# A fused transformer layer with self and cross attention: where the row maxima stand in a hand-written order

## The chip, the cores and the metric

The kernel runs on one core of a Trainium2 chip. The metric is the device time of one execution in microseconds, the median of several runs. The engines that matter here: TensorE (PE) multiplies matrices into PSUM banks, VectorE (DVE) and ScalarE (ACT) read the banks, GpSimd (POOL) works on small SBUF tiles, and SyncE (SP) issues all DMAs in one queue. Each engine runs its own instructions in order and waits on semaphores.

## What is computed

A layer on 16 sequences of 112 rows with 256 features, and 16 source sequences of 375 rows. There are 16 heads of 16 features. The reference, cut down:

```python
x = _layernorm(tgt, ln1_g, ln1_b)
q, k, v = (_heads(t) for t in jnp.split(x @ sa_wqkv, 3, axis=-1))
wei = jnp.einsum('bhtd,bhsd->bhts', q, k) * scale
wei = jnp.where(causal[None, None], wei, NEG_INF)
wei = jnp.where(tgt_padding_mask[:, None, None, :], NEG_INF, wei)
wei = jax.nn.softmax(wei, axis=-1)
sa_out = _merge(jnp.einsum('bhts,bhsd->bhtd', wei, v)) @ sa_wproj + sa_bproj
result = tgt + sa_out
xq = _layernorm(result, ln2_g, ln2_b)
xs = _layernorm(src, ln2_g, ln2_b)
k2, v2 = (_heads(t) for t in jnp.split(xs @ ed_wkv, 2, axis=-1))
q2 = _heads(xq @ ed_wq)
wei2 = jax.nn.softmax(jnp.einsum('bhtd,bhjd->bhtj', q2, k2) * scale, axis=-1)
ed_out = _merge(jnp.einsum('bhtj,bhjd->bhtd', wei2, v2)) @ ed_wproj + ed_bproj
result = result + ed_out
h = jax.nn.relu(_layernorm(tgt, ln3_g, ln3_b) @ ff_w1 + ff_b1)
result = result + (h @ ff_w2 + ff_b2)
```

## The kernel before

The 16 sequences are worked off in 4 groups of 4. Each group has 8 units of attention: units 0 to 3 are the self attention of its four sequences, units 4 to 7 the cross attention of the same four. The units follow each other in the order 2, 3, 4, 5, 0, 1, 6, 7, where 0 and 1 belong already to the next group; so the program repeats one period per group, with a start in front and a last group without successors behind.

A unit has four quarters of four heads. A quarter's scores are one bank of PSUM for a self unit (112 keys) and three for a cross unit (three chunks of 125 keys). The scores leave PE with their row maximum already subtracted: the maximum is computed first, from a separate pass of matmuls, and enters the score matmul as extra rows of the stacked operands. The steps of the order, by their names in the code:

- `max`: PE multiplies into one of three banks `mxb` (four heads at once for a self unit, L1011 and L1015; one head for a cross unit, L1018), and DVE reduces the bank to negated maxima `negm` (L845 self, L848 cross). A self unit has 4 such steps, a cross unit 16. PE waits for DVE when it comes back to a bank (`MAX_BANKS` is 3).
- `max_parts`: POOL splits the maxima of half a unit (8 heads) into three bf16 parts, in four small operations that depend on each other (L638, L640, L642, L644), once the half's last maximum is reduced.
- `mT`: PE transposes these parts into a bank of `misc` (L1062), and ACT copies them, spread over the columns, into `q1st` or `q2st` (L710, 0.91 us each).
- `score` (L1029, L1034), the exponential on ACT into `prob` (L719), `pv`, the weighted sum (L1050), `ot`, its copy by ACT (L726), then `o1` (a transpose, L1057, divided by DVE into `att`, L852 and L854), `o2` (a transpose, L1068, copied by ACT into `aT`) and `o3` (the output projection, L1086, added on DVE; for a cross unit it is followed by the store).
- `qk1`, `q2`, `k2`: projections in three matmul passes twice (L936, L937, L938). The result is split into three bf16 parts, the first on ACT (L704), the other two by three DVE operations (L782 into `rem`, L784, L786). SP then stacks them with 6 DMAs per half (`stack_q1`, `stack_q2`, `stack_k2`). `v1`, `v2`: value projections, copied by ACT.
- `sT`, `xT`, `xq`: transposes of normalised rows (`xs`, `xn`, `xr`), stored as a high part by ACT and a low part by DVE (L775, L832). `stats...` and `norm...` are the layer norms, on DVE with two POOL operations between. `ff1` and `ff2` are the feed-forward matmuls (L1079 for the second).
- `load_tb` and `resid`: the residual's rows come by DMA and POOL adds a bias (L628); `o3` of a self unit adds onto them on DVE (L865).

All steps but scores, maxima and weighted sums use the two banks `misc` in turn, in the order of the steps (`misc_bank`). So a step waits for the reader of the last but one step of this kind.

The order is written by `period_steps`. `other_work` is a table: for each quarter (unit, quarter) a list of other steps. For every quarter three lists are dealt out in turn: its own scores with the weighted sum of the quarter before and an `mT` whose parts are ready; maxima ahead; and the other work. Before, the maxima beside a quarter are those of the quarter four further on, that is of the next unit:

```python
ahead = maxima(*quarters[(n + LEAD) % len(quarters)])
heads = [g] if u < BG else range(4 * g, 4 * g + 4)
```

So a cross unit's sixteen maxima stand four to a quarter beside the unit in front, also where that is a self unit with a single score per quarter: unit 4's beside unit 3, unit 6's beside unit 1. A self unit's four maxima stand one to a quarter. `program_steps` lays the periods behind each other and gives each step the group that it belongs to. Every engine goes through the same list and issues its part of each step.

## Time and profile before

| | us |
|---|---|
| median of 3 runs | 630.61 (628.57 to 631.55) |
| the profiled execution, its own time | 630.3 |
| its span in the trace | 628.4 |

The trace gives every instruction's start and duration on its engine and, for an idle time of an engine, the instruction elsewhere that ended it. Matmuls overlap, so the time that a step takes PE is read from its start to the next start. Units were placed by the order of the instructions: in the second period the first halves or quarters named below run from 211.25 (unit 7), 235.64 (unit 2), 248.96 (unit 3), 273.07 (unit 4), 285.89 (unit 5), 306.88 (unit 0), 321.66 (unit 1), 334.18 (unit 6) and 352.74 (unit 7 again).

### The profile page before, as it was taken

The page shows a single profiled execution, that of the slowest core. Times are in us where ns is not written, and L with a number is a line of the kernel's source. Part 1 is how long each engine was busy: PE and PEld are TensorE (multiplying, and loading weights), DVE is VectorE, ACT ScalarE, POOL GpSimd, SP SyncE. Part 2 cuts the span into 40 slices and gives each one's busy share as a digit, 9 for nine tenths or more (in the row PEclk, how much of TensorE's full clock was granted, in tenths as well). Part 3 has the DMA queues.
Part 4 walks back from the last instruction along what each step waited for, and adds up shares of the span by engine and source line. Part 5 has one row for each costly group of instructions (what it writes and reads, how often), then busy time and mean ns, then how long its engine had stood idle before and what let it go on. Part 6 is the DMA issues. An engine that isn't in the chain of part 4 may idle for free.

```text
span 628.4 us, 14141 instructions
## 1 busy us (share of the span) xinstructions
PE 553.9 (88%) x5564; PEld 448.0 (71%) x5564; DVE 415.1 (66%) x982; ACT 325.3 (52%) x613; POOL 128.9 (21%) x370
## 2 busy tenths in 40 slices
PE   3497899898999999898998999898999999989896
PEld 3395577776877777777876777776877777767664
DVE  5975376788557656698557656698558654685571
ACT  2141646446645756447635756446635655376173
POOL 6800222113103212113112212113112211030010
PEclk9997999999999999999999999999999999999998
DMA  8297018596562038395481039295670058104910
GB/s 244 75 125 141 4 34 128 97 113 72 112 121 64 2 85 132 56 130 66 109 128 47 1 88 131 55 126 68 113 126 20 8 96 131 40 2 79 117 15 16
DMA packets 73122, 52.08 MB, mean 83 GB/s; under 512 B 21920, under 2 KB 72288, under 8 KB 73056
## 3 DMA queue, kind: packets, MB, share of 16 engines
q1 hardware_dynamic: 73056, 51.17, 49.2%
q8 instruction: 44, 0.72, 0.6%
q14 instruction: 22, 0.18, 0.1%
HBM read 14.36 MB, written 1.84 MB: 26 GB/s over the span
## 4 chain that ended last, share of the span: by engine, by line
PE 53%; DVE 26%; ACT 9%; issue 5%; DMA 4%; POOL 3%; SPq 1%; DVEq 0%; POOLq 0%; ACTq 0%
DVE negm L848 8%; PE misc L936 7%; PE misc L1079 7%; PE pvb L1050 6%; PE misc L938 5%; PE scb L1034 5%; PE misc L937 5%; DVE rem L782 3%; PE misc L1086 3%; DMA tb<-in_x 3%; PE mxb L1018 3%; ACT prob L719 2%; ACT qkp L704 2%; DVE stats L758 1%; PE misc L1057 1%
## 5 line engine op out<-in xcount | busy, mean ns | idle before, releaser
L719 ACT ACTIVATE prob<-scb 125x448 f32<-125x448 f32 (+1 forms) x256 | 134.1, 543 | 66.8 <-PE scb L1034 63.0
L848 DVE TENSOR_REDUCE negm<-mxb 112x1 f32<-112x375 f32 x256 | 128.8, 539 | 24.2 <-PE mxb L1018 22.5
L1018 PE MATMUL mxb<-k2st,q2st 96*112 96x375 bf16 x256 | 82.2, 337 | 5.6 <-DVE negm L848 5.1
L1034 PE MATMUL scb<-q2st,k2st 128*125 128x112 bf16 x768 | 74.7, 223 | 4.9 <-ACT prob L719 4.2
L1034 PEld LDWEIGHTS scb<-q2st,k2st 128*125 128x125 bf16 x768 | 64.8, 137 | 17.7 <-ACT prob L719 9.7
L638 POOL CAST mparts<-negm 112x8 bf16<-112x8 f32 x64 | 12.2, 191 | 313.2 <-DVE negm L845 159.6
L845 DVE TENSOR_REDUCE negm<-mxb 112x4 f32<-112x448 f32 x64 | 39.4, 618 | 45.8 <-PE mxb L1015 45.8
L704 ACT ACTIVATE qkp<-misc,bcol 128x224 bf16<-128x224 f32 (+2 forms) x64 | 35.6, 558 | 62.9 <-PE misc L938 51.7
L1050 PE MATMUL pvb<-prob,v 125*17 125x112 f32 (+1 forms) x2048 | 65.0, 261 | 0.1
L782 DVE SCALAR_TENSOR_TENSOR rem<-misc,bcol,qkp 128x224 f32<-128x224 f32 (+2 forms) x64 | 37.5, 587 | 40.4 <-ACT qkp L704 39.7
L1079 PE MATMUL misc<-wf,hT 128*112 128x256 f32 x256 | 59.6, 380 | 0.9 <-DVE rem L782 0.9
L1050 PEld LDWEIGHTS pvb<-prob,v 125*17 125x17 f32 (+1 forms) x2048 | 44.2, 97 | 15.2 <-issue 11.4
L1079 PEld LDWEIGHTS misc<-wf,hT 128*112 128x112 f32 x256 | 44.4, 177 | 11.4 <-DVE rem L782 2.1
L1018 PEld LDWEIGHTS mxb<-k2st,q2st 96*112 96x112 bf16 x256 | 32.1, 130 | 19.2 <-DVE negm L848 13.0
L710 ACT ACTIVATE q1st<-misc 24x896 bf16<-24x896 f32 x32 | 29.1, 910 | 21.1 <-PE misc L1062 20.6
L689 ACT ACTIVATE hT<-misc,bcol 128x448 f32<-128x448 f32 x32 | 20.3, 635 | 32.8 <-PE misc L938 32.8
L710 ACT ACTIVATE q2st<-misc 24x896 bf16<-24x896 f32 x32 | 29.1, 910 | 15.2 <-PE misc L1062 14.5
L936 PE MATMUL misc<-wv_hi,xsT_hi 128*125 128x256 f32 x96 | 31.4, 328 | 5.1 <-DVE rem L782 3.6
L786 DVE TENSOR_TENSOR qkp<-rem,qkp 128x224 bf16<-128x224 f32 (+2 forms) x64 | 34.0, 531 | 2.2
L698 ACT ACTIVATE v<-misc 125x256 f32<-125x256 f32 x48 | 18.5, 385 | 26.4 <-PE misc L938 26.0
L1034 PEld LDWEIGHTS scb<-q1st,k1st 128*112 128x112 bf16 x256 | 23.6, 132 | 5.8 <-issue 0.2
L617 POOL TENSOR_TENSOR veps<-mv,epst 112x1 f32<-112x1 f32 (+2 forms) x36 | 7.0, 194 | 100.8 <-DVE mv L762 100.8
(149 smaller groups left out, 1206.1 us busy)
## 6 DMA issues: line engine op xcount, KB each, us to landing
k2st<-qkp SPq DMA_DIRECT2D x192, 93.8 KB, 4.5
xs<-in_ctx SPq DMA_DIRECT2D x16, 375.0 KB
q1st<-qkp SPq DMA_DIRECT2D x48, 112.0 KB, 5.6
k1st<-qkp SPq DMA_DIRECT2D x48, 112.0 KB, 7.6
q2st<-qkp SPq DMA_DIRECT2D x96, 56.0 KB, 2.2
xn<-in_x SPq DMA_DIRECT2D x4, 448.0 KB, 7.2
tb<-in_x SPq DMA_DIRECT2D x8, 224.0 KB, 9.6
out<-ostage SPq DMA_DIRECT2D x16, 112.0 KB, 4.5
```

The costliest lines, as they stand in the source:

```text
L704: nc.scalar.activation(parts_of(s)[:, 0, 0:n], misc_bank(s)[:, 0:n], ACT.Identity, bias=bcol[:, col:col + 1]).then_inc(s_p1, 1)
L710: nc.scalar.activation(rows, bank[NROW:NROW + 3 * HH, 0:T].unsqueeze(1).broadcast_to([3 * HH, HH, T]), ACT.Copy).then_inc(s_read["act"], 1)
L719: nc.scalar.activation(prob[0:rows, n % PROB_SLOTS, :], scb[n % SCORE_BANKS][0:rows, 0:GH * T], ACT.Exp, scale=SCALE).then_inc(s_ex, 1)
L782: V.scalar_tensor_tensor(r[:, 0:n], bank[:, 0:n], bias, parts[:, 0, 0:n], ALU.add, ALU.subtract).then_inc(s_read["dve"], 1)
L786: V.tensor_tensor(parts[:, 2, 0:n], r[:, 0:n], parts[:, 1, 0:n], ALU.subtract).then_inc(s_p3, 1)
L845: V.tensor_reduce(negm[:, at, i * GH:(i + 1) * GH], mx[0:T, 0:GH * T].rearrange("p (h s) -> p h s", h=GH), axis=AX_X, op=ALU.max, negate=T ...
L848: V.tensor_reduce(negm[:, at, i:i + 1], mx[0:T, 0:S], axis=AX_X, op=ALU.max, negate=True).then_inc(s_mx, 1)
L936: M(dst, w_hi[:, k], x_hi[:, k], start=(k == 0), stop=False)
L1018: mm = M(mx[0:T, 0:S], q2st[0:NROW, i, b * T:(b + 1) * T], k2st[k2_place(q, b)][0:NROW, i, 0:S], start=True, stop=True)
L1034: mm = M(sc[0:rows, j * T:(j + 1) * T], ks, (q1st if u < BG else q2st)[:, h, b * T:(b + 1) * T], start=(u >= BG), stop=(u >= BG or j == GH ...
L1050: mm = M(pvb[32 * j:32 * j + VW, g * T:(g + 1) * T], vals, prob[0:rows, slot, j * T:(j + 1) * T], start=(c == 0), stop=(c == chunks(u) - 1))
L1079: mm = M(bank[0:T, 0:C], hT[:, f, b * T:(b + 1) * T], wf2[:, f, :], start=(f == 0), stop=(f == FT - 1))
```

## The change

A table `MAXIMA_BESIDE` takes the place of `LEAD`: for each unit and quarter it names the unit whose maxima stand there, and which. The self units' maxima stand two to a quarter beside the cross unit in front of the pair: all eight of units 0 and 1 beside unit 5, all eight of units 2 and 3 beside unit 7. The sixteen maxima of unit 4 stand two to a quarter beside units 2 and 3, those of unit 6 beside units 0 and 1. Units 5 and 7 keep theirs beside 4 and 6.

With it, other work moves. `o2` and `o3` of unit 7 go from the end of the period into the first quarter of unit 2 of the next (`o2_late`, `o3_late`, with `of_period` giving them the right group). In unit 7 the projection `q2` comes ahead of `sT`, each K projection is followed by its stack sooner, and `ff1` 3 stands last. In unit 5 the first K projection moves ahead of `xq` 3.

```diff
-LEAD = 4
+MAXIMA_BESIDE = {2: ((4, 0, 1), (4, 2, 3), (4, 4, 5), (4, 6, 7)), 3: ((4, 8, 9), (4, 10, 11), (4, 12, 13), (4, 14, 15)),
...
-        (2, 0): [("load_tb", 1), [("sT", 1, 0), ("sT", 1, 1)]],
+        (2, 0): [("o2_late", 7), ("load_tb", 1), [("sT", 1, 0), ("sT", 1, 1)], ("o3_late", 7)],
...
-        (5, 0): [[("sT", 2, 0), ("sT", 2, 1)], ("xq", 3), ("stats_s", 3)],
-        (5, 1): [("q2", 1, 0), ("stack_q2", 1, 0), ("o1", 4), ("k2", 2, 0), ("stack_k2", 2, 0), ("q2", 1, 1), ("stack_q2", 1, 1), ("k2", 2, 1), ("stack_k2", 2, 1)],
+        (5, 0): [[("sT", 2, 0), ("sT", 2, 1)], ("k2", 2, 0), ("xq", 3), ("stack_k2", 2, 0), ("stats_s", 3)],
+        (5, 1): [("q2", 1, 0), ("stack_q2", 1, 0), ("o1", 4), ("q2", 1, 1), ("stack_q2", 1, 1), ("k2", 2, 1), ("stack_k2", 2, 1)],
...
-        (7, 0): [[("sT", 0, 0), ("sT", 0, 1)]],
-        (7, 1): [("q2", 0, 0), ("stack_q2", 0, 0), ("o1", 6), ("q2", 0, 1), ("stack_q2", 0, 1), ("k2", 0, 0), ("ff1", 3), ("k2", 0, 1)],
+        (7, 0): [("q2", 0, 0), ("stack_q2", 0, 0), [("sT", 0, 0), ("sT", 0, 1)], ("q2", 0, 1)],
+        (7, 1): [("k2", 0, 0), ("stack_k2", 0, 0), ("stack_q2", 0, 1), ("o1", 6), ("k2", 0, 1), ("stack_k2", 0, 1), ("ff1", 3)],
         (7, 2): [("o2", 6), ("stats_s", 1), ("v2", 0, 0), ("v2", 0, 1)],
-        (7, 3): [("o3", 6), [("stack_k2", 0, 0), ("stack_k2", 0, 1)], ("norm_s", 1), ("v2", 0, 2), ("load_src", 2)],
+        (7, 3): [("o3", 6), ("norm_s", 1), ("v2", 0, 2), ("load_src", 2)],
...
     def maxima(u, g):
-        heads = [g] if u < BG else range(4 * g, 4 * g + 4)
-        return [[("max", u, i)] for i in heads] + ([[("max_parts", u, g // 2)]] if g % 2 else [])
+        of, *numbers = MAXIMA_BESIDE[u][g]
+        half = 2 if of < BG else H // 2
+        return [[("max", of, i)] for i in numbers] + ([[("max_parts", of, numbers[-1] // half)]] if (numbers[-1] + 1) % half == 0 else [])
...
-            ahead = maxima(*quarters[(n + LEAD) % len(quarters)])
+            ahead = maxima(u, g)
...
-    s += [("pv", u, 3, c) for c in range(chunks(u))] + [("ot", u), ("v1", 2), ("o1", u), ("v1", 3), ("o2", u), ("o3", u)]
+    s += [("pv", u, 3, c) for c in range(chunks(u))] + [("ot", u), ("v1", 2), ("o1", u), ("v1", 3)]
...
+    def of_period(t, R):
+        kind, *rest = t
+        if kind == "load_tgt":
+            return ("load_tgt", R + 1, *rest)
+        if kind.endswith("_late"):
+            return (kind[:-len("_late")], R - 2, *rest)
+        return (kind, R if t in head else R - 1, *rest)
```

Line numbers behind the table are 14 higher in the changed kernel (L1018 becomes L1032, L1062 becomes L1076). Three places of the order follow.

PE in unit 3 of the second period, round `mT` of unit 4's first half. Before, with `mparts` written by POOL, `att` by DVE, `aT` not yet needed:

```order
L1029 MATMUL scb0<-maskt,identb 112x448
L1034 MATMUL scb0<-q1st,k1st 112x112 x4
L1018 MATMUL mxb2<-k2st0,q2st 112x375
L1068 MATMUL misc1<-ident,att 128x112 x2
L1062 MATMUL misc0<-identb,mparts0 24x112
L1018 MATMUL mxb0<-k2st0,q2st 112x375
L936 MATMUL misc1<-xT_hi,wqk_hi 128x448
```

and now, a quarter earlier:

```order
L952 MATMUL misc0<-xT_hi,wf1_lo 128x448
L1076 MATMUL misc1<-identb,mparts0 24x112
L1043 MATMUL scb1<-maskt,identb 112x448
L1048 MATMUL scb1<-q1st,k1st 112x112 x4
L1032 MATMUL mxb1<-k2st0,q2st 112x375
L1071 MATMUL misc0<-ident,ot 112x128 x4
L1032 MATMUL mxb2<-k2st0,q2st 112x375
```

The `mT` moved from behind `o2` in the third quarter to behind a hidden projection in the first, while its maxima moved a whole unit forward.

PE in unit 0, behind the second K projection of unit 3 of the group before (`k2`, then `v2`). Before:

```order
L938 MATMUL misc0<-xsT_hi,wk2_lo 128x376
L1029 MATMUL scb0<-maskt,identb 112x448
L1034 MATMUL scb0<-q1st,k1st 112x112 x4
L1011 MATMUL mxb2<-identb,maskt 112x448
L1015 MATMUL mxb2<-k1st,q1st 112x112 x4
L1062 MATMUL misc1<-identb,mparts0 24x112
L936 MATMUL misc0<-wv2_hi,xsT_hi 125x256
```

and now:

```order
L952 MATMUL misc0<-xsT_hi,wk2_lo 128x376
L1043 MATMUL scb0<-maskt,identb 112x448
L1048 MATMUL scb0<-q1st,k1st 112x112 x4
L1032 MATMUL mxb2<-k2st0,q2st 112x375
L1032 MATMUL mxb0<-k2st0,q2st 112x375
L950 MATMUL misc1<-wv2_hi,xsT_hi 125x256
```

The `mT` is gone from here, so the value projection writes the other bank of `misc`, and two cross maxima stand where one self maximum stood.

DVE in unit 7, first half, behind the first self maximum. Before, with `rem` and `qkp` the splits of `q2` (128x224) and `k2` (128x375), and `rden`, `att` those of `o1`:

```order
L845 TENSOR_REDUCE negm<-mxb2 112x4
L782 SCALAR_TENSOR_TENSOR rem<-misc1,bcol,qkp 128x224
L784 CAST qkp<-rem 128x224
L786 TENSOR_TENSOR qkp<-rem,qkp 128x224
L852 RECIPROCAL rden<-misc0 112x16
L854 TENSOR_TENSOR att<-misc0,rden 112x256
L782 SCALAR_TENSOR_TENSOR rem<-misc1,bcol,qkp 128x224
L784 CAST qkp<-rem 128x224
L786 TENSOR_TENSOR qkp<-rem,qkp 128x224
L782 SCALAR_TENSOR_TENSOR rem<-misc0,bcol,qkp 128x375
```

and now:

```order
L796 SCALAR_TENSOR_TENSOR rem<-misc1,bcol,qkp 128x224
L798 CAST qkp<-rem 128x224
L800 TENSOR_TENSOR qkp<-rem,qkp 128x224
L859 TENSOR_REDUCE negm<-mxb0 112x4
L796 SCALAR_TENSOR_TENSOR rem<-misc1,bcol,qkp 128x375
L798 CAST qkp<-rem 128x375
L800 TENSOR_TENSOR qkp<-rem,qkp 128x375
L859 TENSOR_REDUCE negm<-mxb1 112x4
L866 RECIPROCAL rden<-misc0 112x16
L868 TENSOR_TENSOR att<-misc0,rden 112x256
L796 SCALAR_TENSOR_TENSOR rem<-misc0,bcol,qkp 128x375
```

The division of `o1` moved from behind one split to behind three (the first stands just above this piece), with the self maxima between them.

## Rows read from the trace of the kernel before

**Rows 1.** of the page: busy time, share of the span and instructions by engine
```profile
PE 553.9 (88%) x5564; PEld 448.0 (71%) x5564; DVE 415.1 (66%) x982; ACT 325.3 (52%) x613; POOL 128.9 (21%) x370
```

**Rows 2.** by windows: stretch, its length, then busy us by engine, granted clock, DMA share
```profile
211.25:223.19 11.94, 11.00 (x124) 9.06 (x125) 8.06 (x20) 7.99 (x16) 1.57 (x8) 1.00 0.10 26
...
256.99:265.54 8.55, 7.46 (x41) 6.16 (x40) 4.89 (x10) 2.72 (x5) 0.79 (x4) 1.00 0.14 45
...
285.89:297.69 11.80, 9.86 (x122) 8.11 (x120) 9.63 (x27) 7.69 (x16) 3.43 (x11) 1.00 0.34 49
```

**Rows 3.** timelines of PE round mT of unit 4: start, us, instruction, [idle before <-releaser]
```profile
119.52 0.21 PE L1062 MATMUL misc<-identb,mparts 112*24 112x112 bf16 x1 [1.25 <-POOL mparts L644]
...
258.99 0.21 PE L1062 MATMUL misc<-identb,mparts 112*24 112x112 bf16 x1 [1.09 <-POOL mparts L644]
...
538.96 0.21 PE L1062 MATMUL misc<-identb,mparts 112*24 112x112 bf16 x1 [1.52 <-POOL mparts L644]
```

**Rows 4.** timeline of PE in unit 0: the V projections of unit 3
```profile
315.09 0.39 PE L936 MATMUL misc<-wv_hi,xsT_hi 128*125 128x256 f32 x1 [1.03 <-DVE rem L782]
...
316.54 0.38 PE L936 MATMUL misc<-wv_hi,xsT_hi 128*125 128x256 f32 x1 [0.28 <-ACT v L698]
```

**Rows 5.** timeline of PE in the last group, units 5 to 6
```profile
580.68 0.62 PE L1057 MATMUL misc<-ident,ot 128*112 128x128 f32 x4 [0.81 <-ACT ot L726]
...
589.75 0.64 PE L1018 MATMUL mxb<-k2st,q2st 96*112 96x375 bf16 x3
...
592.00 1.03 PE L1086 MATMUL misc<-wpe,aT 128*112 128x256 f32 x4
...
596.64 0.32 PE L1018 MATMUL mxb<-k2st,q2st 96*112 96x375 bf16 x1
...
598.30 0.41 PE L936 MATMUL misc<-wv_hi,xsT_hi 128*125 128x256 f32 x1
```

**Rows 6.** by form, DVE: line, tiles, shapes, count | busy us, mean ns | idle before
```profile
L848 DVE TENSOR_REDUCE negm<-mxb 112x1 f32<-112x375 f32 x256 | 128.8, 539 | 24.2 <-PE mxb L1018 22.5
L845 DVE TENSOR_REDUCE negm<-mxb 112x4 f32<-112x448 f32 x64 | 39.4, 618 | 45.8 <-PE mxb L1015 45.8
L782 DVE SCALAR_TENSOR_TENSOR rem<-misc,bcol,qkp 128x375 f32<-128x375 f32 x32 | 19.4, 608 | 22.6 <-ACT qkp L704 22.0
```

**Rows 7.** timeline of PE in unit 3, second quarter: transpose behind o1
```profile
255.02 0.60 PE L951 MATMUL misc<-ident,xn 112*128 112x112 f32 x4 [0.63 <-DVE att L854]
```

**Rows 8.** timeline of DVE at the end of unit 1: residual sum
```profile
336.22 0.42 DVE L865 TENSOR_TENSOR tb<-misc,tb 112x256 f32<-112x256 f32 x1 [2.48 <-POOL tb L628]
```

**Rows 9.** timeline of PE, end of unit 7 and start of unit 2
```profile
234.71 1.09 PE L1086 MATMUL misc<-wpe,aT 128*112 128x256 f32 x4 [0.54 <-ACT aT L712]
...
237.77 0.43 PE L971 MATMUL misc<-ident,xs 125*128 125x125 f32 x2 [0.55 <-ACT q1st L710]
```

**Rows 10.** timeline of DVE in unit 7, first half
```profile
212.40 0.38 DVE L832 TENSOR_TENSOR xq_lo<-misc,xq_hi 128x224 fp32r<-128x224 f32 x1
...
213.24 1.24 DVE L775 TENSOR_TENSOR xsT_lo<-misc,xsT_hi 128x375 fp32r<-128x375 f32 x2
...
218.90 0.42 DVE L854 TENSOR_TENSOR att<-misc,rden 112x256 f32<-112x256 f32 x1
```

**Rows 11.** timeline of PE in unit 5: second K projection
```profile
296.54 0.44 PE L936 MATMUL misc<-xsT_hi,wk_hi 128*128 128x376 f32 x1 [0.62 <-DVE rem L782]
```

**Rows 12.** by windows at the start, columns as in rows 2
```profile
60.00:63.00 3.00, 3.00 (x18) 2.69 (x17) 0.62 (x1) 0.77 (x2) 0.78 (x4) 0.50 0.34 114
```

**Rows 13.** timeline of PE at the start: one self maximum, then mT
```profile
62.85 0.58 PE L1011 MATMUL mxb<-identb,maskt 112*112 112x448 bf16 x1
...
63.59 0.22 PE L1062 MATMUL misc<-identb,mparts 112*24 112x112 bf16 x1
```

**Rows 14.** timeline of SyncE's queue: issues of a K stack
```profile
229.75 8.88 SPq L543 DMA_DIRECT2D k2st<-qkp  x12
```

**Rows 15.** by tile, k2st: time from issue to landing
```profile
DMA to landing us min/median/max: 3.3/4.7/7.4
```

More of the change, by code:

```diff
@@ L52 @@
 FF2_PIECES = 2
-LEAD = 4
+MAXIMA_BESIDE = {2: ((4, 0, 1), (4, 2, 3), (4, 4, 5), (4, 6, 7)), 3: ((4, 8, 9), (4, 10, 11), (4, 12, 13), (4, 14, 15)),
+                 4: tuple((5,) + tuple(range(4 * g, 4 * g + 4)) for g in range(4)), 5: ((0, 0, 1), (0, 2, 3), (1, 0, 1), (1, 2, 3)),
+                 0: ((6, 0, 1), (6, 2, 3), (6, 4, 5), (6, 6, 7)), 1: ((6, 8, 9), (6, 10, 11), (6, 12, 13), (6, 14, 15)),
+                 6: tuple((7,) + tuple(range(4 * g, 4 * g + 4)) for g in range(4)), 7: ((2, 0, 1), (2, 2, 3), (3, 0, 1), (3, 2, 3))}
 MISC_READER = {"xT": "dve", "qk1": "dve", "v1": "act", "ff1": "act", "sT": "dve", "k2": "dve", "v2": "act", "ff2": "dve",
@@ L158, in of_next @@
         if kind in ("max", "max_parts", "mT", "score", "pv", "ot", "o1", "o2", "o3", "stats2", "norm2", "xq"):
-            return t[1] in (0, 1) or (t[1] == UNITS[0] and kind in ("max", "max_parts", "mT") and at[t] > len(s) // 2)
+            return t[1] in (0, 1) or (t[1] in UNITS[:2] and kind in ("max", "max_parts", "mT") and at[t] > len(s) // 2)
         if kind in ("q2", "stack_q2"):
@@ L173, in program_steps @@
     steps, head = period_steps(kt)
-    placed = [("load_tgt", 0)] + [(t[0], R + 1 if t[0] == "load_tgt" else R if t in head else R - 1) + t[1:]
-                                  for R in range(groups + 1) for t in steps]
+    def of_period(t, R):
[5 more added lines that the diff above has]
+        return (kind, R if t in head else R - 1, *rest)
+    placed = [("load_tgt", 0)] + [of_period(t, R) for R in range(groups + 2) for t in steps]
     return [t for t in placed if 0 <= t[1] < groups]
```

## The prediction

> **What bounds the kernel now.** I read the page's busy rows first [rows 1]: TensorE (PE) is busy 88% of the span, VectorE (DVE) 66%. What to see is that no other engine comes near, and that the change can only act on the gaps of TensorE, since it adds and removes no arithmetic. Next the table by stretches [rows 2]: in the steady part a period of about 140 us repeats three times, and its stretches differ. In the third quarter of unit 3 (256.99 to 265.54) PE is busy 7.46 of 8.55 us while DVE works only 4.89; in the first half of unit 5 (285.89 to 297.69) PE is busy 9.86 of 11.80 and DVE 9.63; in the first half of unit 7 (211.25 to 223.19) DVE has 8.06 of 11.94. So DVE is no bound on average but is close to one in the two halves to which the change adds self maxima. Last the timelines round PE's longest waits [rows 3 to 5, 7 to 11]: who releases PE, and how long it stood.
>
> **The change, part by part.** The program's matmuls, reductions, exponentials and DMAs keep their number and shapes, so each term is a wait that goes or comes. The sum is made on the profiled execution's own time, 630.3 us (span 628.4 and 1.9 around it), which lies 0.3 us under the median of 630.61.
>
> 1. *Unit 4's first eight maxima are ready sooner.* Before, the matmul that turns the parts of unit 4's maxima (mT) stands only a score, one maximum and o2 behind the eighth of these maxima, and PE waits for the last of four POOL operations: 1.25, 1.09, 1.09 and 1.52 us, once in each group (the two middle ones alike, one is shown) [rows 3]. Afterwards the eight maxima end in the last quarter of unit 2, and unit 3's first score, a weighted sum and a hidden projection stand between, which lies over the POOL chain of four operations. What is late next is qk1, whose operands are ready. Gain 4.9 us; 3.5 if DVE's norm1, which now comes behind the eighth maximum, is taken to delay it.
>
> 2. *Unit 0, behind unit 3's K projections.* Before, mT takes a bank of misc between the second K projection and the first V projection, so V needs the bank that DVE's rem operation reads last: 1.03 us, then 0.28 for the next one, in three groups [rows 4]. Afterwards mT stands a unit earlier, V takes the other bank, and only the transpose behind V meets the later rem. PE arrives there some 0.6 us before DVE is done, so about half of 1.31 stays; leaving out the order of banks, the bounds are a gain of 0 and of 1.31 each. I take 0.8 three times: 2.4.
>
> 3. *Last group.* Before, with no work of a next group, unit 6's sixteen maxima stand nearly bare: the first six take PE from 589.75 to 592.00, at DVE's pace, and five later ones with mT from 596.64 to 598.30 [rows 5]. Afterwards six of them stand in unit 5's tail, where PE waits 0.81 us for ot and again for rem anyway. The first cluster falls from 2.25 us to nothing, the second from 1.66 to about 1.1: gain 2.8. Bounds: 0.5 (DVE, at 539 ns a maximum [rows 6], becomes late for the rems) to 3.5.
>
> 4. *Residual's landing.* At the end of unit 1, DVE waits for the sum that POOL makes of a DMA just landed: 2.48 us in one group [rows 8], and less in the two others. Between that load and its reader three fewer cross maxima stand afterwards (1.1 us less cover on PE), but as DVE also has no maximum left to do behind it, PE may run about 1.7 us further, until its three maximum banks are full. I take a gain of 0.6 in two of the three groups, rounded up for the third: 1.3. Bounds: loss 2, gain 2.5.
>
> 5. *o2 and o3 of unit 7 moved into the next unit.* PE's wait for aT goes (0.54 us, and some 0.3 of waiting that the overlap of matmuls hides in the row), three times. In exchange o2 and o3 now share two misc banks with mT and two transposes; the second transpose waited 0.55 us for the 0.91 us copy of mT before [rows 9], and now the first one also waits for aT and o3 for the first one's xsT_lo: about 0.6 more. Net gain 0.2 each: 0.6, bounds ±2.
>
> 6. *Fewer maxima at a time in units 1, 2 and 3.* DVE does 8 cross maxima in unit 3 instead of 16, so norm1, att and rem stand less behind them. The two behind o1 in unit 3 show in [rows 7] as 0.63 for att and a shorter one; with others like them in the three units I take 0.8 a group: 2.5, rounded up. Bounds 0 and 4.5.
>
> 7. *Unit 7's first half, the price.* Two more self maxima, at 618 ns on DVE each, and two stacks' projections sooner [rows 6]. The q2 projection now comes right behind the first maximum, at 211.9, and needs xq_lo, which DVE ends at 212.78 [rows 10]: 0.9 us. Its second half wants the bank that xsT_lo frees, 0.8 later. The second K projection wants the bank of att, and att now stands behind two splits for q2, one for K and three self maxima. DVE's queue from 214.2 on, added up: q2 split 1.1, maximum 0.6, two xsT_lo 1.2, q2 split 1.1, maximum 0.6, K split 1.5, maximum 0.6, rden and att 0.7 [rows 6, 10], where a split's cast and subtraction together are taken at one and a half times its rem operation: 7.4, and 1.5 of standing for ScalarE's first parts, so 223.1. PE comes at 221.8: 1.3 to 1.4. Walked through to its end with these durations, the half ends at 225.3 instead of 223.19; 0.8 of that is the two maxima's own matmuls, which unit 2 no longer has. Net loss 1.3, three times: 3.9. Bounds: 0 to 8.
>
> 8. *Unit 5's first half, the price.* Two more self maxima in a stretch where DVE has 9.63 of 11.80 [rows 2]. The wait of 0.62 for rem [rows 11] is replaced by a like one; xq and q2 come 0.5 later behind the K split, and the bank of o1 some 0.6 later behind DVE's queue; walked through, the half ends at 299.5 instead of 297.69, of which 0.95 is work moved here. Net loss 0.85, three times: 2.5. Bounds 0 to 5.
>
> 9. *Start.* All eight self maxima of units 0 and 1 before the first score. From 60 to 63 PE's granted clock is 0.50, 1.2 GHz of its 2.4, behind a stretch in which it had little to do; at that clock a self maximum takes PE 0.74 us from start to next start (62.85 to 63.59) [rows 12, 13], more than DVE's 618 ns, so that the new order, which by the same adding up would save 2 us at full clock, saves 0.6. Bounds: ±2.
>
> Sum: −4.9 −2.4 −2.8 −1.3 −0.6 −2.5 +3.9 +2.5 −0.6 = −8.7, and 630.3 − 8.7 = 621.6.
>
> The new waits are many and short. In the stretches of rows 2 the granted clock stays at 1.00, although PE stands there for up to 1.09 us at a time [rows 2, 3]. The Trainium skill (TensorE: Matmul & The Clock Gate, "A second HAM failure mode: psum-queue depth-cycling") says that frequent micro-idles between groups of matmuls can make the clock fall and rise again; this trace does not show it. By that rule the new waits of unit 7 could bring it about; that is one of the rivals.
>
> **The rivals.**
> - *Waits only move to DVE.* In units 5 and 7 the queue is longer than I added up, so terms 7 and 8 cost double: +6.4, 628.0 us. For: DVE's 9.63 of 11.80 [rows 2], and every delay there is queued in front of the next reader of a bank. Against: the quarters behind them have slack, and DVE's idle share is over 30% in unit 7.
> - *The losses don't come.* A wait of PE for one engine overlaps one for another, so terms 7 and 8 vanish and the rest stays: 615.2.
> - *Slower: unit 4's stack lands too late.* The first cross maximum now comes at about 236.9 instead of 249.36. Before, twelve issues for that stack ran from 229.75 over 8.88 us, and a landing takes 3.3 to 7.4 us [rows 14, 15]. Afterwards its first half is issued from about 222, behind six issues of a q stack, and has landed by 226 + 7.4 = 233.4, 3.5 us early. It decides once the K split ends more than 3.5 us later, or a landing doubles under the loads. A maximum 4 us late would stop PE in four places: +16, 637.6 us.
> - *The clock falls.* A stretch at 0.50 like the start's [rows 12] in unit 7 of each of three groups, taken at twice the 3 us shown, would cost half its length: +9 to +10, 631.7. Against: no stretch of rows 2 shows one.
> - *Nothing moves in effect:* the order shows every place changed, so this needs gains and prices that cancel: 630.3.
>
> **How the numbers follow.** Forecast 0.55 (616 to 627); waits moved to DVE 0.22; losses absent 0.10; late stack 0.07; clock 0.03; nothing 0.03. The time is the forecast's 621.6. The range takes in the first three cases nearly whole, with the bounds of terms 3, 7 and 8: 612.5 to 630, leaving out late stack, clock and the ends of the others, some 0.2. A change of 0.5% is about what a measurement of this kernel can tell: 3.2 us, faster below 627.5. Faster: 0.55 + 0.10 + 0.05 of the second = 0.70; same: 0.17 + 0.03 + 0.02 = 0.22; slower 0.08.
>
> **What would show it.** Right: mT of unit 4 has no wait for POOL; V behind unit 3's K projections waits under 0.1 us; from ff2 of the last group to unit 6's first score is 2 to 3 us shorter; in unit 7's first half a K projection waits over 1 us for att. Wrong: the first cross maximum of unit 4 waits for a DMA; PE's share of unit 5 falls under 80%; the clock row of the page shows a second low stretch; DVE waits over 3 us for POOL's residual.

## The result: slower by 1.1%, and the profile after

The changed kernel takes 637.41 us (median; 634.59 to 640.44), the kernel before 629.59 in the same series; the ratio is 1.0113, with a 95% interval of 1.0077 to 1.0148. The forecast was 621.6 us, and faster. The profiled execution of the changed kernel has a span of 635.2 us, 6.8 more than before.

The page of the changed kernel, its busy time by engine and the granted clock in 40 slices:

```profile
PE 551.2 (87%) x5564; PEld 445.9 (70%) x5564; DVE 416.9 (66%) x982; ACT 324.8 (51%) x613; POOL 132.6 (21%) x370
...
PEclk9966898999999999999999999999999999999999
```

Against [rows 1] PE is busy 2.7 us *less*: no work was added, and the loss of 6.8 us is standing time of PE. The same stretches as in [rows 2], by windows of the changed kernel (stretch, length, busy us of PE, PEld, DVE, ACT, POOL, granted clock, DMA share): first half of unit 7, third quarter of unit 3, first half of unit 5.

```profile
216.37:231.18 14.81, 11.85 (x134) 9.91 (x135) 9.35 (x23) 8.72 (x17) 2.33 (x12) 1.00 0.20 48
265.09:271.88 6.79, 6.79 (x39) 5.86 (x38) 3.13 (x6) 1.81 (x4) 0.00 (x0) 1.00 0.13 44
292.07:306.15 14.08, 11.13 (x133) 9.08 (x131) 11.50 (x31) 8.58 (x17) 4.12 (x15) 1.00 0.53 76
```

What to see: unit 3's quarter fell from 8.55 to 6.79 us and PE no longer stands in it at all. Unit 7's half rose from 11.94 to 14.81 and unit 5's from 11.80 to 14.08. The first half of unit 7 was given 25.3 - 23.2 = 2.1 us more by the prediction; it took 2.9. The waits that it named are there, in the timeline of PE (start, us, instruction, idle before and its releaser):

```profile
218.05 0.34 PE L950 MATMUL misc<-xq_hi,wq_hi 128*128 128x224 f32 x1 [0.84 <-DVE xq_lo L846]
...
222.00 0.37 PE L950 MATMUL misc<-xq_hi,wq_hi 128*128 128x224 f32 x1 [0.71 <-DVE xsT_lo L789]
...
228.84 0.44 PE L950 MATMUL misc<-xsT_hi,wk_hi 128*128 128x376 f32 x1 [1.22 <-DVE att L868]
```

What the prediction did not have stands in the first group. There unit 7's projections and self maxima run with no unit 7 beside them, between unit 1's last score and unit 2's first. This stretch, before and after, by windows:

```profile
72.24:95.86 23.62, 21.20 (x165) 17.19 (x163) 16.30 (x45) 10.61 (x22) 6.50 (x14) 1.00 0.12 30
```

```profile
72.72:102.44 29.72, 23.72 (x186) 19.53 (x184) 19.30 (x52) 12.52 (x24) 8.99 (x26) 0.97 0.25 50
```

It is 6.1 us longer, of which 1.6 is four self maxima moved here from unit 2, and some 0.9 is the granted clock (an estimate: 3% of 29.7 us at 0.97). PE's timeline there, and POOL's queue behind its longest wait:

```profile
87.49 0.37 PE L950 MATMUL misc<-xq_hi,wq_hi 128*128 128x224 f32 x1 [1.19 <-DVE xsT_lo L789]
...
91.30 0.44 PE L950 MATMUL misc<-xsT_hi,wk_hi 128*128 128x376 f32 x1 [0.86 <-DVE rem L796]
...
99.82 0.21 PE L1076 MATMUL misc<-identb,mparts 112*24 112x112 bf16 x1 [1.88 <-POOL mparts L658]
```

```profile
97.66 0.85 POOL L633 TENSOR_TENSOR rstd<-veps,mhalf 125x3 f32<-125x3 f32 x1
98.47 0.19 POOL L652 CAST mparts<-negm 112x8 bf16<-112x8 f32 x1
...
99.42 0.25 POOL L658 TENSOR_TENSOR mparts<-mrem,mparts 112x8 bf16<-112x8 f32 x1
```

The POOL wait that the change removed in unit 3 has a new place: the parts of unit 3's maxima are queued behind `rstd`, which waits for DVE's statistics, which stand behind two maxima; and PE has nothing to do there but V projections that come before `mT`.

Where the 6.8 us went, by the starts of the units' first scores in both traces: up to unit 1's last score +0.5; to unit 2 +6.1; units 2 and 3 of the first group -2.9; then, summed over three passes each, units 7, 2 and 3 +2.9, and units 4, 5, 0, 1 and 6 +1.5; from the last group's unit 4 on -1.4.

### The profile page after: what moved, and what is told of

It reads as the page before. It is cut to its first block, busy times and chain, and to the rows that moved or that the text cites. A ratio compares the mean times of both kernels' runs of the same rounds, so it can differ in the third digit from the quotient of the medians.

```text
span 635.2 us, 14143 instructions
## 1 busy us (share of the span) xinstructions
PE 551.2 (87%) x5564; PEld 445.9 (70%) x5564; DVE 416.9 (66%) x982; ACT 324.8 (51%) x613; POOL 132.6 (21%) x370
## 4 chain that ended last, share of the span: by engine, by line
PE 53%; DVE 23%; ACT 10%; DMA 5%; issue 4%; SPq 3%; POOL 2%; DVEq 0%; POOLq 0%; ACTq 0%
PE misc L950 8%; PE misc L1093 7%; PE pvb L1064 7%; PE misc L952 6%; PE misc L951 5%; DVE negm L862 5%; PE scb L1048 5%; DVE rem L796 4%; PE mxb L1032 3%; PE misc L1100 3%; DMA tb<-in_x 3%; ACT qkp L718 2%; ACT prob L733 2%; SPq L557 2%; DVE qkp L800 2%
## 5 line engine op out<-in xcount | busy, mean ns | idle before, releaser
L862 DVE TENSOR_REDUCE negm<-mxb 112x1 f32<-112x375 f32 x256 | 130.7, 540 | 43.8 <-PE mxb L1032 41.2
L1032 PE MATMUL mxb<-k2st,q2st 96*112 96x375 bf16 x256 | 82.8, 336 | 1.9 <-DVE negm L862 1.7
L718 ACT ACTIVATE qkp<-misc,bcol 128x375 bf16<-128x375 f32 (+2 forms) x64 | 35.6, 558 | 73.8 <-PE misc L952 62.4
L652 POOL CAST mparts<-negm 112x8 bf16<-112x8 f32 x64 | 16.7, 261 | 269.3 <-DVE negm L862 166.9
L796 DVE SCALAR_TENSOR_TENSOR rem<-misc,bcol,qkp 128x375 f32<-128x375 f32 (+2 forms) x64 | 37.5, 586 | 47.8 <-ACT qkp L718 47.4
L1064 PE MATMUL pvb<-prob,v 125*17 125x112 f32 (+1 forms) x2048 | 66.4, 263 | 0.6 <-ACT prob L733 0.2
L1093 PE MATMUL misc<-wf,hT 128*112 128x256 f32 x256 | 58.1, 380 | 1.4 <-DVE rem L796 1.4
L1032 PEld LDWEIGHTS mxb<-k2st,q2st 96*112 96x112 bf16 x256 | 32.4, 130 | 11.9 <-DVE negm L862 6.5
L800 DVE TENSOR_TENSOR qkp<-rem,qkp 128x375 bf16<-128x375 f32 (+2 forms) x64 | 33.9, 530 | 2.2
L1025 PE MATMUL mxb<-identb,maskt 112*112 112x448 bf16 x64 | 25.3, 395 | 7.3 <-DVE edb L940 2.8
```

The costliest lines, as they stand in the source:

```text
L718: nc.scalar.activation(parts_of(s)[:, 0, 0:n], misc_bank(s)[:, 0:n], ACT.Identity, bias=bcol[:, col:col + 1]).then_inc(s_p1, 1)
L796: V.scalar_tensor_tensor(r[:, 0:n], bank[:, 0:n], bias, parts[:, 0, 0:n], ALU.add, ALU.subtract).then_inc(s_read["dve"], 1)
L800: V.tensor_tensor(parts[:, 2, 0:n], r[:, 0:n], parts[:, 1, 0:n], ALU.subtract).then_inc(s_p3, 1)
L862: V.tensor_reduce(negm[:, at, i:i + 1], mx[0:T, 0:S], axis=AX_X, op=ALU.max, negate=True).then_inc(s_mx, 1)
L1032: mm = M(mx[0:T, 0:S], q2st[0:NROW, i, b * T:(b + 1) * T], k2st[k2_place(q, b)][0:NROW, i, 0:S], start=True, stop=True)
L1064: mm = M(pvb[32 * j:32 * j + VW, g * T:(g + 1) * T], vals, prob[0:rows, slot, j * T:(j + 1) * T], start=(c == 0), stop=(c == chunks(u) - 1))
```

## Experiments

**The two halves of the edit, and the two pairs.** The work order alone (every maximum as before):

```diff
-MAXIMA_BESIDE = {2: ((4, 0, 1), ...), 3: ..., 5: ..., 0: ..., 1: ..., 7: ...}
+MAXIMA_BESIDE = {2: ((3, 0), (3, 1), (3, 2), (3, 3)), 3: tuple((4,) + tuple(range(4 * g, 4 * g + 4)) for g in range(4)), ...}
```

> The other work of the changed kernel (unit 7's and unit 5's projections in the new order, o2 and o3 of unit 7 in the next unit), with every maximum placed as before. Theory M (the price comes from the two extra self maxima standing in the same half as the projections, because each takes DVE time and holds up the reader of the next misc bank): unit 7's first half in the steady part lies near before's 11.9 us plus at most 0.7, the waits for POOL in units 3 and for the V projection in unit 0 come back, and the whole is 630 to 633 us. Rival W (the new order of the projections alone is the price: q2 in front of the transposes, K ahead of the second stack): the first half of unit 7 stays at 14 us or so as in the changed kernel, the gains in units 3 and 0 are missing, and the whole is 639 to 644 us.

Measured: 636.95 us, ratio 1.0088 (1.0058 to 1.0119). This is between the two ranges. For the whole, theory M falls: without a single moved maximum the kernel is as slow as the changed one. Its first halves of units 7 and 5, and two of the waits in unit 7:

```profile
209.29:222.26 12.97, 10.92 (x124) 9.08 (x125) 8.74 (x22) 7.70 (x16) 1.55 (x8) 1.00 0.15 36
285.50:298.28 12.78, 9.99 (x120) 8.24 (x119) 9.94 (x28) 7.67 (x16) 3.32 (x11) 1.00 0.44 70
```

```profile
210.97 0.34 PE L954 MATMUL misc<-xq_hi,wq_hi 128*128 128x224 f32 x1 [0.84 <-DVE xq_lo L850]
...
214.62 0.37 PE L954 MATMUL misc<-xq_hi,wq_hi 128*128 128x224 f32 x1 [0.81 <-DVE xsT_lo L793]
```

Each half is 1.0 us longer than before with the same work in it, and rival W's 14 us for unit 7's half is not reached either. Of the 2.9 us that this half grew by in the changed kernel, the order makes 1.0; with the maxima alone (next run) it is 13.54 us, 1.6 longer, of which 0.8 is moved work. So both halves of the edit have a price there. By rows of this execution, the span of 635.1 is made up of before's 628.4, +4.7 in units 7 and 2, +3.2 in unit 5, +2.2 in the last group's unit 5 and +1.7 in its unit 3, in both of which the granted clock fell, +0.7 between the first group's unit 1 and unit 2, -3.1 in unit 6's first quarters, -2.5 by an earlier first score, and -0.2 in the rest.

The maxima alone:

```diff
-        (7, 0): [("q2", 0, 0), ("stack_q2", 0, 0), [("sT", 0, 0), ("sT", 0, 1)], ("q2", 0, 1)],
+        (7, 0): [[("sT", 0, 0), ("sT", 0, 1)]],
...
-        (7, 3): [("o3", 6), ("norm_s", 1), ("v2", 0, 2), ("load_src", 2)],
+        (7, 3): [("o3", 6), [("stack_k2", 0, 0), ("stack_k2", 0, 1)], ("norm_s", 1), ("v2", 0, 2), ("load_src", 2)],
```

> All maxima placed as in the changed kernel, but the other work as before, so that the K stack of unit 4 is issued in unit 7's last quarter, near 230 us, while the first cross maximum for it stands in unit 2's first quarter. If the sooner stacks are needed, TensorE stands for a DMA at the first cross maximum of unit 4, 5 to 10 us in each of four groups: 650 to 670 us. Rival (stacks land in time anyway, and theory W holds): no DMA wait over 1 us there, and the whole is under before, 622 to 628 us, since it has all gains and no reordered projections.

Measured: 632.07, ratio 1.0031 (1.0001 to 1.0062). Neither number is met. The stacks land in time even when issued late: over the whole trace PE waits for them twice, 2.0 us in all, both times in the last group (by tile, `k2st`):

```profile
who waited for it (us, times):
  PE mxb L1032: 2.0, 2
```

So "stacks filled sooner" bought almost nothing, and the order it needed cost 1.0 us a half. In the steady part the moved maxima of units 2 to 4 about cancel (unit 7 +3.0, units 2 and 3 -2.9), and those of units 0, 1 and 6 gain 0.65 a group. What keeps the whole above before is the first group's stretch, 29.78 us here as well, with a POOL wait of 2.94 in it. With the work order alone it was 24.30, so the price of the first group comes mostly with the self maxima that stand there, not with the order:

```profile
97.48 0.21 PE L1076 MATMUL misc<-identb,mparts 112*24 112x112 bf16 x1 [2.94 <-POOL mparts L658]
```

The change in units 7, 2, 3 alone, and in units 5, 0, 1 alone (table rows and work of the other pair as before):

> The change in units 7, 2 and 3 alone (self maxima of units 2 and 3 beside unit 7, o2 and o3 of unit 7 late, unit 4's stack sooner); units 5, 0 and 1 as before. From the rows of the changed kernel: unit 7's first half costs 1.9 us net three times, the same stretch of the first group, where nothing stands beside it, 4.5 net (6.1 longer, 1.6 of it moved work), unit 2 some 0.3 each, and unit 3 gives back 1.0 four times: 5.7 + 4.5 + 1.0 - 4.0 = +7, 634 to 638 us. If this half of the change is not to blame: under 631 us.

Measured: 635.89, ratio 1.0090 (1.0059 to 1.0121), inside its range.

> The change in units 5, 0 and 1 alone (self maxima of units 0 and 1 beside unit 5, unit 2's first K projection in unit 5's first quarter, unit 6's maxima spread over units 0 and 1); units 7, 2 and 3 as before. From the rows of the changed kernel: unit 5's first half +1.3 net three times, unit 0 -1.0 three times, unit 1 -0.3 three times, the last group's tail -2: 4.0 - 3.0 - 0.9 - 2.0 = -2, 626 to 630 us. If this half costs as much as the other: over 632 us.

Measured: 631.34, ratio 1.0036 (0.9997 to 1.0075), 1.3 us over before where a gain was expected within 626 to 630; why it missed was not followed. Together the two make the whole loss (+5.8 and +1.3 against +7.8); four fifths of it is the pair of units 7, 2 and 3.

**The first group's order undone.** The list of steps is taken from the kernel before up to unit 4's first score in the first group:

```diff
+    a, b = program_steps_a(kt, groups), program_steps_b(kt, groups)
+    first = ('score', 0, 4, 0, 0)
+    return b[:b.index(first)] + a[a.index(first):]
```

> The changed kernel, with the order of the kernel before up to the first score of unit 4 of the first group, and its own order from there. Theory F: a fixed price is paid once, in the first group, where unit 7's stretch has no unit 7 beside it: from its first maximum to unit 2's first score the changed kernel took 19.8 us against 13.7, of which 1.6 is moved work and 2.9 is given back in units 2 and 3. The stretch is then 13.7 again and the whole 3 to 4 us shorter than the changed kernel's 637.4: 633.5 to 634.5 us. Rival (the start of this execution was slow for its low clock alone, by chance): the whole stays within 1 us of the changed kernel, 636.5 to 638.5.

Measured: 634.34 us, ratio 1.0092 (1.0063 to 1.0121), inside theory F's range, 3.1 under the changed kernel. The two medians come from different series, each with its own runs of before (629.41 and 629.59), and the intervals of the two ratios overlap; the difference of 3.1 alone would not show the theory. The stretch does: it is 23.6 us with the order of before there, as in the kernel before, and 29.6 to 29.8 in the changed kernel, the run with the maxima alone and that with units 7, 2 and 3 alone.

**Two `mT` steps moved, nothing else.**

```diff
+MOVED = ((('mT', 4, 0), ('qk1', 2)), (('mT', 1, 0), ('v2', 3, 1)))
...
+    for t, behind in MOVED:
+        s.remove(t)
+        s.insert(s.index(behind) + 1, t)
```

> The kernel before, in which only two mT steps move later in their quarter: that of unit 4's first half from behind o2 of unit 2 to behind the last qk1 of the quarter, and that of unit 1's first half from in front of unit 3's V projections to behind them. Theory G (the gains of terms 1 and 2 need no other place of the maxima): the wait for POOL in unit 3 (1.09 to 1.52 us, four times) and the wait of V for rem in unit 0 (1.31 in all, three times, about half of it kept) go: 630.1 - 4.9 - 2.4 = 622.8, taken with 623 to 626. Rival (other waits take their place, since the quarters' length is set by DVE's maxima and splits): 629 to 631.

Measured: 625.68, ratio 0.9910 (0.9869 to 0.9952). Theory G holds, inside its range, with no maximum moved. The whole gains 3.7 us, half of the 7.3 that terms 1 and 2 promised. The third and the fourth quarter of unit 3:

```profile
257.41:264.79 7.38, 7.38 (x42) 6.05 (x40) 4.80 (x10) 1.86 (x5) 0.79 (x4) 1.00 0.16 50
264.79:272.93 8.14, 7.47 (x39) 5.87 (x39) 6.48 (x13) 3.31 (x5) 0.00 (x0) 1.00 0.79 109
```

The third went from 8.55 to 7.38; the fourth gave 0.6 back (7.52 before). Unit 0's third quarter went from 4.40 to between 3.31 and 3.35 and gave nothing back. By the rows, units 3 and 0 together gain 6.1 us in this execution, and unit 6's first quarters, where the residual is waited for, take 4.0 of it away: 7.35, 6.45 and 5.92 us in place of 4.35, 6.37 and 4.96. The residual's load lands there in 7.0 to 7.5 us; before it did in 5.4 to 7.4.

**o2 and o3 of unit 7 late, alone** (the rest as before).

```diff
-        (2, 0): [("load_tb", 1), [("sT", 1, 0), ("sT", 1, 1)]],
+        (2, 0): [("o2_late", 7), ("load_tb", 1), [("sT", 1, 0), ("sT", 1, 1)], ("o3_late", 7)],
```

> The kernel before, with o2 and o3 of unit 7 moved into unit 2's first quarter and nothing else. If the price read in the run with the other work alone is this step's (unit 7's last quarter 8.57 to 7.03 us, unit 2's first 2.51 to 4.59, together +0.54 a group): +0.5 three times, 631 to 632 us. If the move is a gain of 0.2 each as forecast: 629.5. If it is the whole price of the new work order in unit 7 (+1.5 a group): 634 to 635.

Measured: 629.92, ratio 0.9993 (0.9959 to 1.0028). From unit 7's last quarter to the end of unit 2's first the trace of this kernel has 11.26 us, that of before 11.08: +0.2 a group, neither the gain of 0.2 nor the loss of 0.5. PE's waits there were 0.54 for `aT` and 0.55 for `mT`'s copy; now they are 0.30, 0.39 and 0.55, for `aT`, that copy and the transposes' low part.

```profile
227.67:238.93 11.26, 10.02 (x115) 7.68 (x115) 4.87 (x14) 7.26 (x14) 1.92 (x6) 1.00 0.57 90
```

**The parts that the rows had shown to gain, together:** the maxima of units 0, 1 and 6 as changed, every projection as before, `mT` of unit 4 late.

> The kernel before with two parts: the maxima of units 0, 1 and 6 placed as in the changed kernel (beside units 5, 0 and 1) while every projection keeps its old place, and mT of unit 4's first half behind the last qk1 of its quarter. From the rows of the run with the maxima alone, units 5, 0 and 1 gain 0.65 a group and the last group's tail 1.3 to 2; the mT step gains 1.1 to 1.5 four times if theory G holds: 630.1 - 2.0 - 1.6 - 4.6 = 622, taken with 621 to 625 us. If theory G falls: 626 to 628.

Measured: 625.01, ratio 0.9911 (0.9882 to 0.9940), at the head of its range. That is no better than the two `mT` steps alone, whose ratio is 0.9910.

**All maxima moved, first group and projections as before.**

> All maxima placed as in the changed kernel, the projections in the order of before, and the first group up to its unit 4 in the order of before throughout. The run with the maxima alone took 632.1 us; the first group's price, 3 to 4 us by the run that undid it, goes: 628 to 629.5 us. If the gains and prices of the maxima cancel in each period as the rows of that run say (unit 7 +3.0, units 2 and 3 -2.9, units 5, 0 and 1 -0.65), it can't come below 627. If the maxima table was a gain throughout and only the start spoilt it: 624 to 626.

Measured: 629.08, ratio 0.9996 (0.9958 to 1.0034). This is inside the first range. With the first group's order and the work order as before, the whole table of maxima is worth nothing measurable.

**The residual's load sooner** (term 4), on the kernel before:

```diff
+MOVED = ((('load_tb', 0), ('score', 0, 3, 0)),)
```

> The kernel before, with the load of the residual's first half issued at the start of unit 0's last quarter, some 7 us sooner, and nothing else. Theory L (term 4's wait is the landing of this load, which POOL's sum waits for with DVE or the parts of unit 6's maxima queued behind it): unit 6's first quarter falls from 4.35, 6.37 and 4.96 us to 4.2 each, 3 us in all: 626.5 to 628 us. Rival (the wait is for POOL's queue or the DMA engines, which an earlier issue doesn't change): 629 to 631.

Measured: 628.16, ratio 0.9954 (0.9920 to 0.9988). Unit 6's first quarter is 4.23 us in all three groups, as expected, but not for the reason expected. SyncE's queue in this kernel, then in the one before:

```profile
327.31 0.32 SPq L558 DMA_DIRECT2D tb<-in_x  x1
327.68 0.36 SPq L563 DMA_DIRECT2D xs<-in_ctx  x1
```

```profile
322.12 0.49 SPq L558 DMA_DIRECT2D xs<-in_ctx  x1
326.96 0.35 SPq L573 DMA_DIRECT2D out<-ostage  x1
327.35 0.43 SPq L553 DMA_DIRECT2D tb<-in_x  x1
```

The load is issued at 327.3 in both. What changed is that the load of source rows (375 KB) now comes behind it and not 5 us ahead of it, and a store of 112 KB behind it as well; which of the two matters was not separated. The residual's load lands in 2.6 us instead of 7.4, and in the two other groups in 3.3 and 2.9 instead of 5.4 and 6.0. By tile `tb`, of this kernel and of before in that stretch:

```profile
DMA to landing us min/median/max: 2.6/2.6/2.6
```

```profile
DMA to landing us min/median/max: 7.4/7.4/7.4
```

**The transposes ahead of q2 again** in unit 7, the rest as changed:

```diff
-        (7, 0): [("q2", 0, 0), ("stack_q2", 0, 0), [("sT", 0, 0), ("sT", 0, 1)], ("q2", 0, 1)],
+        (7, 0): [[("sT", 0, 0), ("sT", 0, 1)], ("q2", 0, 0), ("stack_q2", 0, 0), ("q2", 0, 1)],
```

> The changed kernel, with the two transposes of unit 7's first quarter ahead of both q2 projections again (as before) and the rest as changed. Theory Q (the price of the new work order in unit 7 is that q2 needs DVE's low part of xq at once, 0.57 us, and that its second half wants the bank of DVE's low part of the transposes, 0.66 to 1.19 us): unit 7's first half falls by about 1 us in each of three groups and in the first: 633 to 634.5 us against 637.4. Rival (it is the K projections and stacks that come sooner, with two splits more in DVE's queue): 636.5 to 638.

Measured: 632.86, ratio 1.0044 (1.0010 to 1.0078), 4.5 us under the changed kernel. Theory Q holds, a little under its range. The half is 13.54 us in place of 14.81; the waits for `xq_lo` and `xsT_lo` are gone but for 0.16, that for `att` stays. The first group's stretch is 27.87 us in place of 29.72, about half of it because the granted clock is 1.00 there in this execution:

```profile
211.48:225.02 13.54, 11.85 (x134) 9.76 (x135) 9.45 (x23) 8.71 (x17) 2.34 (x12) 1.00 0.19 48
```

```profile
222.68 0.44 PE L950 MATMUL misc<-xsT_hi,wk_hi 128*128 128x376 f32 x1 [1.22 <-DVE att L868]
```

**The mix with three more moves.**

```diff
+MOVED = ((('mT', 4, 0), ('qk1', 2)), (('load_tb', 0), ('score', 0, 3, 0)), (('mT', 0, 0), ('k2', 2, 1)), (('mT', 3, 0), ('v2', 1, 1)))
```

> The mixed kernel (625.0 us: maxima of units 0, 1 and 6 as changed, projections as before, mT of unit 4 late) with three more moves: the residual's load sooner, mT of unit 0's first half behind unit 2's second K projection, and mT of unit 3's first half behind unit 1's second V projection. If the waits add up one by one: -3.0 for the load, -0.6 three times and -0.4 four times: 625.0 - 6.4 = 618.6, taken with 618 to 621 us. If the removed waits come back at the next bank: 623 to 625.

Measured: 623.04, ratio 0.9873 (0.9814 to 0.9931): between the two cases. The load's move brought unit 6's first quarter to 4.11 us; the two moves of `mT` brought their waits back at the next bank: in unit 5 the 1.20 us for `rem` at q2 became 0.50, 0.17 and 0.40 for later ones, and unit 2's third quarter went from 5.89 to 6.13.

**Three prices undone together** (first group, transposes first, unit 5's order), the rest as changed:

> The changed kernel with three things undone together: the first group's order up to its unit 4, the transposes ahead of q2 in unit 7, and unit 5's projections in the order of before. If the prices found one by one add up: q2's place 4.5 us, of which 1.5 lies in the first group and is counted there, the first group 3.1 to 3.7, unit 5's order 1.0 three times: 637.4 - 3.0 - 3.4 - 3.0 = 628, taken with 626.5 to 629. If they overlap (each wait hides another): 631 or more.

Measured: 626.91, ratio 0.9956 (0.9926 to 0.9986), inside its range. The prices add up, and what remains of the change is a gain of 0.4%.

**Unit 5's order alone**, on the kernel before:

```diff
-        (5, 0): [[("sT", 2, 0), ("sT", 2, 1)], ("xq", 3), ("stats_s", 3)],
+        (5, 0): [[("sT", 2, 0), ("sT", 2, 1)], ("k2", 2, 0), ("xq", 3), ("stack_k2", 2, 0), ("stats_s", 3)],
```

> The kernel before, with unit 5's projections in the changed order and nothing else (the first K projection of unit 2 and its stack in unit 5's first quarter). By the rows of the run with the other work alone, unit 5's first half goes from 11.8 to 12.8 us in each of three groups and in the last group too by about 1: 629.5 + 3 to 4 = 632.5 to 633.5. If that price belonged to the other moves: within 1 us of 629.5.

Measured: 630.36, ratio 1.0017 (0.9984 to 1.0051): a miss by 2 us. The first half of unit 5 is 12.78 us, 1.0 longer, as in the first experiment, and in the last group it is 13.64 in place of 11.39, with a fall of the clock in it. But unit 6's first quarter is 4.20 us in every group, where before had 4.35, 6.37 and 4.96:

```profile
283.80:296.58 12.78, 9.99 (x121) 8.24 (x119) 9.94 (x28) 7.67 (x16) 3.32 (x11) 1.00 0.47 72
...
333.08:337.28 4.20, 3.94 (x56) 3.04 (x54) 3.44 (x9) 2.20 (x5) 1.53 (x6) 1.00 0.00 0
```

The residual's load lands in 3.7 us here instead of 7.4, so that much of the price comes back at the landing. This is no single chance: the run with the work order alone has this order of unit 5 too, and 4.21 us in all three groups, while in the four traces with unit 5 and its maxima as before (before, `mT` late, o2 late, pair 7, 2, 3) the quarter varies from 4.20 to 7.35. Why the load lands sooner is only argued: part of a stack's traffic lies earlier. In the changed kernel, with the maxima moved too, this return is missing (5.3, 5.6 and 4.9 us), and the landing in the same group takes 6.3.

**The fastest version:** the mix and the residual's load, without the two moves of `mT`.

```diff
+MOVED = ((('mT', 4, 0), ('qk1', 2)), (('load_tb', 0), ('score', 0, 3, 0)))
```

> The mixed kernel with the residual's load sooner, without the two further moves of mT that the last version had (their rows: unit 2's third quarter 5.89 to 6.13, unit 5's second and third together 13.2 to 13.7, so that each gave back more than it took away). If rows add up: 623.0 - 0.24 x 4 - 0.47 x 3 = 620.7, taken with 620 to 622 us. If such differences of rows don't carry over to the whole: 623.

Measured: 619.92 us, ratio 0.9853 (0.9795 to 0.9911), just under the foot of its range and the lowest median of all. Its interval overlaps that of the run above with 623.04, and both profiled executions have a span of 620.4, so that which of the two is faster is not shown. It is 5.1 us under the mix alone, in whose trace unit 6's first quarters took 5.97, 5.42 and 5.04 us; here each takes 4.11.

## Why the prediction was wrong, point by point

1. *Unit 4's first mT, -4.9:* right. All four POOL waits of [rows 3] are gone. In the timeline of the changed kernel `mT` stands at 260.65 with no idle time before it:

```profile
260.65 0.22 PE L1076 MATMUL misc<-identb,mparts 112*24 112x112 bf16 x1
```

2. *Unit 0, -2.4:* right. The quarter of [rows 4] stood 1.31 us in waits, now 0.54: -0.8 three times, as forecast.

3. *Last group, -2.8:* the sign is there (from ff2 to unit 6's first score 13.50 us before, 10.46 after), but the quarter ahead of it grew by 0.9, where the maxima went: -2.1.

4. *Residual's landing, -1.3:* nothing came. Unit 6's first quarters sum to 15.7 us before and after. The term was argued from cover; the load-order run shows that what is issued in front of the load decides its landing. In the changed kernel the source rows' load stands 1.9 to 3.3 us ahead of it, and it lands in 5.7 to 6.3 us.

5. *o2 and o3 late, -0.6:* alone it is +0.2 a group, +0.5 in all. The waits that came were as large as those that went and 0.15 more, where they were added up to 0.2 less.

6. *Fewer maxima in units 1, 2 and 3, -2.5:* about nothing. The wait of [rows 7] for `att` is gone, but the V projection behind it waits for the transposes' low part; PE's two waits in that quarter sum to 0.86 us before and 0.87 after:

```profile
264.27 0.38 PE L950 MATMUL misc<-wv_hi,xsT_hi 128*125 128x256 f32 x1 [0.75 <-DVE xT_lo L789]
```

7. *Unit 7's first half, +3.9:* the mechanism was right to the wait (1.22 for `att` where 1.3 to 1.4 was added up), the size was not: 2.1 net a group, +6.2. Of this, 1.3 a group is q2 ahead of the transposes. And **this is the step that failed**: the price was multiplied by three, for the three groups with a unit 7 beside the work. The first group's copy of these steps was taken at nothing without naming what covers it. Nothing does. Net of moved work that stretch cost 4.5 us, the largest single miss of the sum, some 0.9 of it by the low clock behind its longest wait. With the order of before there the stretch is 23.6 us again and the whole lower by 3.1.

8. *Unit 5's first half, +2.5:* 2.28 - 0.95 moved work = 1.3 a group, +4.0. The order alone makes 1.0 of it. It was multiplied by three as well, and the last group's copy left out, where no self maxima are added but the order is new. It cost 1.0 us more: from unit 5's first score to its third quarter 11.39 us before, 12.38 after.

```profile
560.35:571.74 11.39, 9.30 (x112) 7.50 (x110) 8.66 (x25) 7.58 (x16) 2.57 (x7) 1.00 0.07 17
```

```profile
568.48:580.86 12.38, 9.17 (x110) 7.55 (x109) 8.90 (x26) 7.67 (x16) 2.56 (x7) 1.00 0.14 33
```

9. *Start, -0.6:* from the first score to unit 1's last the changed kernel took 9.60 us, before 10.13; the same order at full clock 8.15 (the maxima-only run), the 2 us named. But the first score came 1.0 us later, so that unit 1's last score is +0.5 in place of -0.6; the first score moves more than that between executions, so this part is chance.

Of the rivals, "waits only move to DVE" named the place of terms 7 and 8, and their doubling; they came to 1.6 times. "Unit 4's stack lands too late" fell: even the stacks issued late cost 2.0 us in two places, and in the changed kernel PE waits for no stack. That its figure, 637.6 us, is almost the measured time is luck. The forecast's sum of losses was short by 3.8 in terms 7 and 8, by 4.5 in the first group and by 1.0 in the last; its gains were too large by 2.5 (term 6), 1.3 (4), 1.1 (5), 1.1 (9) and 0.7 (3). That is 16.0, where the forecast -8.7 and the spans' +6.8 lie 15.5 us apart; the 0.5 between them has no name here.

All four signs of being right were seen: no POOL wait at that `mT`, no wait of V behind unit 3's K projections, 3.0 us less from ff2 to unit 6's first score, and 1.22 us for `att`. They tested the gains and one price, and none of them the two ends of the program. Of the signs of being wrong one came, the second low stretch in the page's clock row, and half of another: PE's share of unit 5 is 79% in its first half, though 87% over the unit.

On the clock: a fall in unit 7 was a rival, and there was none; the granted clock is 1.00 in unit 7's first half in all three groups, though PE stands there three times for 0.7 to 1.2 us. It fell to 0.50 in the first group, from 100.5 to 103.9, behind the wait of 1.88 us. The rule of the Trainium skill (TensorE: Matmul & The Clock Gate, "A second HAM failure mode: psum-queue depth-cycling"), by which frequent short idles between groups of matmuls make the clock fall and rise, is thus not borne out in unit 7. In the last group's unit 5 it may be: four waits of 0.55 to 0.99 us in a row were followed by a fall in three executions and not in two (last section).

## What to carry to other kernels

A software pipeline's first and last passes run the same steps without their cover: cost a moved step once for the steady part and once for each end (here 4.5 us in the first group and 1.0 in the last, both priced at nothing). Try first to move the one step that waits on a late engine (two `mT` steps here, -0.9%) and then the work it waits for. In this kernel a projection must not stand in front of the transposes whose low part frees its bank. A gain ahead of a DMA landing can be lost at it: moving `mT` alone gave 3.7 us where its rows had gained 6.1, and the load had to be moved too. A saved wait counts only after the next reader of the same two banks has been followed: of the four moves of `mT` tried here, three gave part or all of it back one bank later.
